# Sums of each half of a head taken earlier, the stacks' transfers first in SyncE's order, and VectorE's key steps behind both maxima

## The reference, cut to what matters

```python
q, k, v = (proj(Wq), proj(Wk), proj(Wv))                # 16 heads of 64
scores = jnp.einsum('bhqd,bhkd->bhqk', q, k)
scores = scores + bias.transpose(2, 0, 1)[None]          # by distance, constant when far
attn = jax.nn.softmax(scores, axis=-1)
ctx = jnp.einsum('bhqk,bhkd->bhqd', attn, v)
return ctx @ Wo.T
```

## Time and profile before

| | us |
|---|---|
| three runs: median (lowest to highest) | 3972.28 (3969.41 to 3975.57) |
| the profiled execution | 3972.34 |
| its span, first to last instruction | 3970.6 |
| TensorE busy | 3727.9 |
| GpSimd busy | 2681.1 |
| VectorE busy | 2466.4 |
| ScalarE busy | 2004.6 |

### The profile page before, as it was taken

One profiled execution on the slowest core, in us unless ns is written; L12 is line 12 of the kernel. 1 busy time (PEld: TensorE's weight loads), 2 busy tenths in 40 slices (PEclk: granted clock), 3 DMA queues, 4 the chain that ended last, 5 costly groups with the idle time before them and its releaser, 6 DMA issues. The chain is left out here.

```text
span 3970.6 us, 64135 instructions
## 1 busy us (share of the span) xinstructions
PE 3727.9 (94%) x21277; PEld 2216.2 (56%) x21277; DVE 2466.4 (62%) x3356; ACT 2004.6 (50%) x3452; POOL 2681.1 (68%) x1402
## 2 busy tenths in 40 slices
PE   8989999999999989999999999999997999997899
PEld 7754444444444444444444444444446888885377
DVE  3466666666666656666666666666635777775632
ACT  3335555555555555555555555555553555553232
POOL 1128888888888878888988888889893343430010
PEclk9989999999999999999999999999998999998999
DMA  7652222432223452222332222332312333335710
GB/s 221 162 120 63 66 64 71 103 75 69 64 64 81 101 153 64 69 64 67 93 90 66 68 64 67 98 84 65 105 36 88 100 106 103 104 116 174 262 46 22
DMA packets 368370, 366.99 MB, mean 92 GB/s; under 512 B 189339, under 2 KB 261531, under 8 KB 362776
## 3 DMA queue, kind: packets, MB, share of 16 engines
q1 hardware_dynamic: 299064, 336.50, 31.6%
q10 hardware_dynamic: 67168, 20.98, 2.2%
q0 software_dynamic: 1920, 6.29, 0.5%
HBM read 142.64 MB, written 89.70 MB: 59 GB/s over the span
## 5 line engine op out<-in xcount | busy, mean ns | idle before, releaser
L354 POOL TENSOR_TENSOR acc<-acc,probs 128x1024 f32<-128x1024 f32 x894 | 2126.4, 2379 | 306.9 <-ACT probs L814 189.3
L939 DVE TENSOR_REDUCE maxes<-ps 128x2 f32<-128x1024 f32 x1024 | 1253.2, 1225 | 607.6 <-PE ps L610 596.7
L817 ACT ACTIVATE probs<-ps,far_bias 128x1024 f32<-128x1024 f32 (+7 forms) x1280 | 997.4, 819 | 795.4 <-DVE near_s L956 546.0
L641 PE MATMUL ps<-probs,v_head 128*64 128x512 f32 x4096 | 1002.1, 610 | 8.9 <-ACT ctx_out L800 6.9
L629 PE MATMUL ps<-stacks 64*128 64x512 f32 x6144 | 825.7, 398 | 1.8 <-ACT probs L814 1.8
L629 PEld LDWEIGHTS ps<-stacks 64*128 64x128 f32 x6144 | 591.0, 188 | 126.9 <-ACT probs L814 7.9
L610 PE MATMUL ps<-stacks 64*128 64x512 f32 x2048 | 508.0, 494 | 142.4 <-DVE maxes L939 56.9
L610 PEld LDWEIGHTS ps<-stacks 64*128 64x128 f32 x2048 | 194.5, 187 | 700.0 <-DVE maxes L939 464.3
L641 PEld LDWEIGHTS ps<-probs,v_head 128*64 128x64 f32 x4096 | 251.0, 137 | 463.0 <-issue 450.9
L956 DVE TENSOR_TENSOR near_s<-ps,near_bias 128x384 f32<-128x384 f32 (+2 forms) x576 | 265.8, 491 | 58.4 <-PE ps L629 55.3
L962 DVE TENSOR_TENSOR c_q<-ps,c_q 64x512 fp32r<-64x512 f32 x128 | 87.5, 684 | 311.2 <-ACT c_q L773 311.2
(11 more groups left out here) (278 smaller groups left out, 4515.4 us busy)
## 6 DMA issues: line engine op xcount, KB each, us to landing
stacks<-c_q SPq DMA_DIRECT2D x128, 256.0 KB, 4.3
stacks<-c_d SPq DMA_DIRECT2D x64, 512.0 KB, 6.9
stacks<-c_k SPq DMA_DIRECT2D x32, 768.0 KB, 5.5
stacks<-c_k SPq DMA_DIRECT2D x64, 384.0 KB, 7.0
scr_v<-probs ACTq DMA_DIRECT2D x32, 512.0 KB, 4.1
v_head<-scr_v SPq DMA_DIRECT2D x32, 512.0 KB, 8.5
scr_ctx<-ctx_out SPq DMA_DIRECT2D x128, 128.0 KB, 2.3
both_ctx<-scr_ctx SPq DMA_DIRECT2D x32, 512.0 KB, 4.0
```

Of the source, the lines that this page charges most:

```text
L354: pool.tensor_tensor(acc[:, qb, :], acc[:, qb, :], pr, ALU.add).then_inc(s["summed"], 1)
L641: mm = pe.matmul(ps[64 * half:64 * half + 64, PV, :], v_head[:, side, kt, :], probs[:, st % PT_RING, half * 512:(half + 1) * 512], start=k ...
L817: ins = act.activation(probs[:, st % PT_RING, a:z], sc[:, a:z], ACT.Exp, bias=bias)
L939: dve.tensor_reduce(maxes[:, qt:qt + HALF_GROUPS // 2 + 1:HALF_GROUPS // 2, first_chunk + pair], ps[:, bank:bank + 2, :], AX.X, ALU.max).t ...
```

## The change

The sums of half 0 are taken in group 9 and not 13, those of half 1 in group 1 of the next head and not 5; reciprocals and contexts move with them. `divisors` is cut in two: `spread` stands for half 1 right behind `fill`, and for half 0, with the divisors, ahead of the guard of the next head. On VectorE `largest` for the second maximum now stands ahead of `step` and `step_lo`.

```diff
-SUM_GROUPS = {13: 0, 5: 1}
-RECIP_GROUPS = {14: 0, 6: 1}
-CONTEXT_STEPS = {31: 0, 15: 1}
+SUM_GROUPS = {9: 0, 1: 1}
+RECIP_GROUPS = {10: 0, 4: 1}
+CONTEXT_STEPS = {25: 0, 13: 1}
...
-            def divisors(n, qb):
+            def spread(n, qb):
                 sp.wait_ge(s["sum_out"], 2 * n + qb + 1)
                 for q in range(QUARTERS):
                     sp.dma_start(part[QP * q:QP * q + QP, :],
                                  sums[QP * q:QP * q + 1, 0:QUARTER].rearrange("o (p c) -> o p c", c=PART)).then_inc(s["spread"], 16)
+            def divisors(n, qb):
                 sp.wait_ge(s["recip"], 2 * n + qb + 1)
...
                 if nxt:
                     fill(n + 1, 1 - side)
+                if carry:
+                    spread(n - 1, 1)
...
                 if h_weights is not None:
                     xn_block(1, reload)
+                if own:
+                    spread(n, 0)
+                    divisors(n, 0)
                 if nxt:
                     guard(n + 1, 1 - side, 0)
...
                 if own:
-                    divisors(n, 0)
                     store_ctx(n, 0)
...
-                    if tb == 1:
+                    if tb == 0:
                         past(pe, s["sum_out"], 2 * (m - 2))
-                    if tb == 3:
+                    if tb == 2:
                         past(pe, s["sum_out"], 2 * (m - 2) + 1)
...
+                    if has_max(n, g):
+                        largest(n, side, g, 1)
                     if prep and g in STEP_GROUPS:
                         step(n + 2, STEP_GROUPS[g])
                     if lowered:
                         step_lo(*lowered)
-                    if has_max(n, g):
-                        largest(n, side, g, 1)
```

## The result

| | before | after |
|---|---|---|
| median of the runs (lowest to highest) | 3972.61 (3969.41 to 3975.57) | 3829.59 (3826.96 to 3832.03) |
| the profiled execution | 3972.34 | 3826.96 |
| its span | 3970.6 | 3825.2 |
| mean granted clock | 0.977 | 0.987 |

The ratio is 0.964, with an interval of 0.9623 to 0.9657: the kernel became 143 us faster. The forecast was 121 us, 3851, and its range ended at 3838. So the sign and the mechanism of its terms were right, the size was not. The lines of TensorE, VectorE and ScalarE stand 7 lower in the kernel after (the maxima are L617 and L946, the scores L636, the values L648), SyncE's loads and stores of the divisors and contexts 3 lower.

The account below looks back on a forecast made before the run. The prediction took TensorE to set the pace, busy 2495.7 of 2630 us in the head loop. Its terms, 49.4 + 12.1 + 55.9 + 3.8 = 121.2 us, came off 3972.34 to give 3851, range 3838 to 3900.

Parts of the forecast that it names:

- waits for the stacks: TensorE's waits for the stacks' transfers at the heads' starts: go with the earlier fill, except head 30's, worth 49.4 us.
- low clock after them: Group 3 at granted clock 0.50 after the stacks' wait, in nine heads: 12.1 us more gained.
- VectorE's order: Second maximum ahead of the step in groups with near steps: TensorE's waits for the maxima go, 55.9 us.
- heads 30 and 31: Last two heads, bound by GpSimd: head 30's 5.1 us keys wait goes, a context costs 1.30 us, net 3.8 us.
- The 14 loop turns stay, and so does the low clock behind half of them: TensorE's turns of the loop over heads: 28.6 us of "issue" waits expected unchanged, so no gain counted.
- The chain from the context's step to the fill to the last keys: SyncE at a head's start: context 0 at step 25 lets the fill start at H - 2.7, keys land H + 12.4.
- VectorE's tie: Group 12 on VectorE: the moved step ends at 1094.98, just when the next reduction would start anyway.
- The signs to the other side: Signs of being wrong: GpSimd releasing ScalarE's exponentials, VectorE waiting for the spread, GpSimd for reciprocals, step's copy ending ScalarE's idle time.
- (a): Rival, chance 0.14: GpSimd becomes the bound, 79.0 against 79.5 us a head; 15 to 57 us back, 3866 to 3908.
- (b): Rival, chance 0.11: VectorE's order gives nothing, the step only moves the wait to the next pair; 3907, half of it 3879.
- (c): Rival, chance 0.05: the fill starts early but the last keys still land late; 3882 if half the wait stays.
- (d): Rival, chance 0.04: half 1's reciprocals come too late for GpSimd, 30 us lost per us late; 4001 at 5 us.

Follow-up runs that it names:

- e1: The kernel before with only VectorE's new order (second maximum ahead of the steps): 3947.99 us, ratio 0.9938.
- e4: The kernel after plus two loads of the reciprocals' size and form, into an unread tile, just ahead of TensorE's loop branch: 3838.77 us, ratio 0.9666.
- e3: The kernel after with the contexts back at steps 31 and 15, sums and reciprocals still early: 3946.72 us, ratio 0.9945.
- e5: The kernel after with every context multiplication of heads 0 to 29 done twice on GpSimd: 3850.47 us, ratio 0.9694.
- e2: The kernel after with VectorE's old order (steps ahead of the second maximum): 3892.85 us, ratio 0.9799.

## Why the prediction was wrong, step by step

Each group's length, from start of scores to start of scores, summed over heads 0 to 29 and compared between the two profiled executions, gives the terms. A group in which the clock fell is counted whole in the rows on low clock, as the forecast did in group 3. Gains in us:

| term | forecast | trace |
|---|---|---|
| waits for the stacks (group 2) | 49.4 | 51.1 |
| low clock after them (group 3, 10 heads) | 12.1 | 14.3 |
| VectorE's order (groups 0, 3, 11, 12, 15) | 55.9 | 54.4 |
| the 13 turns, idle | 0 | 5.3 |
| low clock behind turns (group 0, 7 heads before, 3 after) | 0 | 7.9 |
| rest of heads 0 to 29 | 0 | 2.3 |
| heads 30 and 31 | 3.8 | 3.8 |
| up to head 0, and behind the attention | 0 | 2.7 and 3.5 |
| sum (before rounding) | 121.2 | 145.4 |

An undisturbed group 0 takes 4.75 us before and 4.14 after. Had the seven slow ones of before been measured against 4.75 and not 4.14, 4.2 of the 7.9 us would stand in VectorE's row.

**The step that failed** is "The 14 loop turns stay, and so does the low clock behind half of them". It is the largest term that was mis-sized, 0 where the trace has 13.2 us (5.3 and 7.9; by the other count 9.0), and the time lies 8.4 us below the range. Three things were wrong in it. First, the idle time of a turn is not a constant of the branch: it fell from 2.06 to 1.65 us in the mean because the divisors' loads no longer go out just ahead of it: e1 keeps the loads and the idle time, and e4 brings both back. The forecast moved those loads and never asked who else was using the queues at that moment. Second, the clock fell behind 3 turns and not 7. One such turn of after, with the clock in the window behind it (columns as in the earlier trace rows):

```profile
985.39 0.49 PE L617 MATMUL ps<-stacks 64*128 64x512 f32 x2 [2.03 <-issue]
...
986.10 1.04 PE L636 MATMUL ps<-stacks 64*128 64x512 f32 x6
...
991.80 1.55 PE L636 MATMUL ps<-stacks 64*128 64x512 f32 x12
```

```profile
986.60:990.00 3.40, 3.40 (x16) 1.93 (x14) 2.09 (x4) 1.73 (x3) 3.09 (x2) 0.50 1.03 316
```

Group 0 takes 991.80 - 986.10 = 5.70 us there and 1071.32 - 1067.18 = 4.14 in head 10, undisturbed: 1.56 us for each. Third, there are 13 turns. The fourteenth "issue" of the earlier trace rows is no turn: it stands in group 3 of head 29, behind the landing of its keys, which went out at 2744.93 (two rows of before, SyncE and TensorE):

```profile
2744.93 2.60 SPq L423 DMA_DIRECT2D stacks<-c_k  x2
```

```profile
2750.29 0.50 PE L610 MATMUL ps<-stacks 64*128 64x512 f32 x2 [1.91 <-issue]
```

2750.29 - 2744.93 is 5.4 us, the landing time that the forecast used (5.2). So 1.9 us belonged to the stacks' term, which explains that term's miss of 1.7.

**The right steps.** The chain from the context's step to the fill to the last keys came out within 0.6 us at each point (fill H - 2.1 for H - 2.7, last keys H + 7.1 for H + 7.2 and landed at H + 12.1 for H + 12.4, spread of half 1 H + 10.5 for H + 11 and landed at H + 18.4 for H + 18, the loads of its reciprocals landed at H + 32.1 for H + 32), and e3 shows that most hangs on it. VectorE's tie held; its term came out 1.5 lower: 89 undisturbed places gave 0.57 us each by the starts ((54.4 - 4.1)/89), where the forecast had 96 at 0.54 and some of these stand in groups at low clock or in the last two heads. The low clock was ten heads, not nine. Heads 30 and 31 came out at 3.8, in part by luck: from 2816 and 2678 us on, TensorE's wait for the stacks there fell from 5.1 to 0.6 us and that for the context's copy from 6.9 to nothing, while its waits for `probs` grew from 3.8 to 8.7.

**The signs to the other side** that the forecast listed as wrong were there without being wrong: ScalarE waits for GpSimd about once a head (1.5 us in the mean, forecast 0.4), and its copy of the step waits 0.95 us in 59 places, but TensorE asks for neither in time to notice, as the forecast argued.

**The rivals.** (a) falls: GpSimd has about 1.8 us a head to spare (e5), though no more. (b) falls: without VectorE's order the time is 3893 (e2). (c) falls: 1.4 us are left of the stacks' wait. (d) falls: GpSimd waited once, 0.5 us, for the divisors.

**What stays open.** The start of head 0 comes 2.7 us earlier; in the five other traces with VectorE's new order it lies at 260.2 to 262.5 us and in e2, with the old one, at 263.6 (264.1 before), so that is probably the order's too. The 3.5 us behind the attention lie inside what traces of the same code differ by: from the first matmul of the last sums (L678 before) to the end, the six experiments take 989.1 to 995.2 us. Nor was it settled which turn is followed by low clock: in the kernel after the clock fell after 1.72 us of idle and not after 1.96, in e4, with turns as long as before, behind 4 of them and not 7, and in e5, with turns as short as after (21.4 us), behind 5. Over all traces it fell behind 7, 9 and 4 turns with the loads there (before, e1, e4), behind 3, 3 and 5 without them (after, e2, e5) and behind none in e3, each in one execution. So the 7.9 us are measured, but that the loads' move brought them is not shown.

## What to carry to other kernels

When a change moves a small transfer, ask at both ends what else runs at that moment: here loads that left the neighbourhood of a loop's branch gave back 5 us of idle time, which the sum had at nothing. When two waits of one engine lie in a row, price them together: the earlier arrival that the first edit gives is paid into the second wait (24 and 79 us apart, 143 together). And a row named "issue" is not yet a loop's turn: count the turns in the code, and look where each one stands.

## What the runs showed of the hardware that was not expected

- A turn of TensorE's loop idles for 2.06 us in the mean with two broadcast loads just ahead of the branch (before; 2.04 in e1, 2.01 in e4), 1.65 with the fill's queries near it (after; 1.66 in e2, 1.65 in e5), and 1.45 in e3, where SyncE's queue is blocked at that point and no transfer of it goes out near the turn (13 turns, 18.8 us).
- The same four spreading transfers take SyncE 2.50 us to issue behind a pause and 5.81 straight behind the fill.
